# Products on 64x64 quarters of TensorE, with 128-row sums in two rounds

## The reference

```python
x = x + conv(_gn(x))          # relu(out_w @ (sigmoid(mask_w x) * relu(info_w x)))
t = tokens(x)
n = _ln_t(t)                  # query, key, value; elu+1; KV = K^T V; message @ Wm; norm
h = relu(concat(n, msg) @ W1) @ W2
t = t + n + layernorm(h)      # attention and MLP
probs = softmax(_ln_t(t) @ gate_w + gate_b)      # top 2 of 8 experts
for e in range(8):
    out += cw[:, e] * (gelu(_ln_t(t) @ W1[e] + b1[e]) @ W2[e] + b2[e])
result = t + out
```

## Time and profile before

| | |
|---|---|
| median of three runs | 1174.82 us (1172.48 to 1178.27) |
| span of the profiled execution | 1171.7 us |
| TensorE matmul busy | 1058.5 us, 90% |
| VectorE, ScalarE, GpSimd busy | 63%, 55%, 31% |
| granted TensorE clock, mean | 0.985 |
| a turn with all stages | 138.2 us |

### The profile page before, as it was taken

One profiled execution on the slowest core, in us unless ns is written; L12 is line 12 of the kernel. 1 busy time (PEld: TensorE's weight loads), 2 busy tenths in 40 slices (PEclk: granted clock), 3 DMA queues, 4 the chain that ended last, 5 costly groups with the idle time before them and its releaser, 6 DMA issues.

```text
span 1171.7 us, 16823 instructions
## 1 busy us (share of the span) xinstructions
PE 1058.5 (90%) x6646; PEld 442.3 (38%) x6646; DVE 740.2 (63%) x1529; ACT 641.8 (55%) x866; POOL 361.7 (31%) x280
## 2 busy tenths in 40 slices
PE   4798589979999899988999899998999989998898
PEld 1453244323533245332453235432453324532232
DVE  5744745686647875587664966468764886556344
ACT  3345355654566556664556546556556555665454
POOL 0000031333323333333232333133332342324465
PEclk9989889999999999999999999999999999999999
DMA  5000086007700284005810068000850039200760
GB/s 157 6 1 1 1 179 149 3 22 173 169 1 19 54 189 104 1 19 112 185 50 1 19 149 198 1 19 19 194 134 1 18 69 201 42 1 19 179 145 23
DMA packets 15597, 88.62 MB, mean 76 GB/s; under 512 B 3488, under 2 KB 6816, under 8 KB 11424
## 3 DMA queue, kind: packets, MB, share of 16 engines
q1 hardware_dynamic: 15520, 87.57, 32.3%
HBM read 78.12 MB, written 9.44 MB: 75 GB/s over the span
## 4 chain that ended last, share of the span: by engine, by line
PE 74%; DVE 12%; ACT 9%; issue 3%; DMA 1%; DVEq 0%; POOL 0%; POOLq 0%; SPq 0%
PE HP L847 15%; PE HP L861 14%; ACT H L992 5%; PE R L646 5%; PE R L621 4%; PE R L610 4%; PE R L699 3%; PE R L717 2%; PE R L708 2%; PE R L786 2%; PE R L795 2%; PE R L788 2%; PE R L861 2%; PE R L675 2%; DVE TM L1355 2%
## 5 line engine op out<-in xcount | busy, mean ns | idle before, releaser
L1044 POOL TENSOR_TENSOR XB<-TM,XB 128x512 f32<-128x512 f32 x254 | 323.0, 1286 | 658.5 <-DVE TM L1355 658.5
L992 ACT ACTIVATE H<-HP,W 128x1024 f32<-128x1024 f32 x224 | 243.0, 1116 | 205.7 <-PE HP L847 205.1
L1355 DVE SCALAR_TENSOR_TENSOR TM<-HP,B2S,CWB 128x512 f32<-128x512 f32 x224 | 163.2, 742 | 207.1 <-PE HP L861 196.3
L847 PE MATMUL HP<-XF,W1E 64*128 64x512 f32 x1024 | 269.9, 630 | 19.3 <-DVE TM L1355 18.5
L861 PE MATMUL HP<-H,W 128*64 128x512 f32 x896 | 233.1, 616 | 18.0 <-ACT H L992 18.0
L847 PEld LDWEIGHTS HP<-XF,W1E 64*128 64x128 f32 x1024 | 84.1, 187 | 143.9 <-DVE TM L1355 71.0
L861 PEld LDWEIGHTS HP<-H,W 128*64 128x64 f32 x896 | 48.5, 135 | 171.2 <-ACT H L992 116.3
L1156 DVE SCALAR_TENSOR_TENSOR BIG<-R,T 128x512 f32<-128x512 f32 x112 | 69.5, 681 | 20.9 <-PE R L610 20.8
L930 ACT ACTIVATE T<-R 128x512 f32<-128x512 f32 x96 | 57.4, 598 | 39.8 <-PE R L646 31.4
L958 ACT ACTIVATE T<-R,MINUS 128x512 f32<-128x512 f32 x64 | 41.4, 688 | 27.3 <-PE R L708 24.4
L1243 DVE SCALAR_TENSOR_TENSOR BIG<-T,R 128x512 f32<-128x512 f32 x64 | 41.8, 684 | 21.6 <-ACT T L958 21.6
(11 more groups left out here) (179 smaller groups left out, 1411.3 us busy)
## 6 DMA issues: line engine op xcount, KB each, us to landing
CWB<-gates_hbm SPq DMA_DIRECT2D x32, 1536.0 KB, 20.4
CWB<-gates_hbm SPq DMA_DIRECT2D x32, 512.0 KB, 6.6
out<-XB SPq DMA_DIRECT2D x15, 512.0 KB, 3.0
X<-x SPq DMA_DIRECT2D x14, 512.0 KB, 3.8
XF<-x SPq DMA_DIRECT2D x2, 512.0 KB, 6.1
gates_hbm<-RT SPq DMA_DIRECT2D x16, 64.0 KB, 1.6
W<-wpack SPq DMA_DIRECT2D x1, 968.0 KB, 4.9
W1E<-w1e SPq DMA_DIRECT2D x1, 512.0 KB, 7.4
```

What stands on the lines that cost most here:

```text
L847: last = mm(HP[u % BATCH][:, half(k)], W1E[img(k), e, :], XF[img(k), 1 - par, s, half(c)], start=True, stop=True)
L992: f(activated(b, u).rearrange("p k t -> p (k t)"), HP[u % BATCH][:, :], ACT.Gelu, bias=col(B1E + e))\
L1044: nc.gpsimd.tensor_tensor(acc, TM[:, u % BATCH, :], acc, ALU.add).then_inc(acc_done, 1)
L1355: v.scalar_tensor_tensor(out=TM[:, u % BATCH, :], in0=sums_of(b, u), scalar=B2S[:, e % 2, e // 2:e // 2 + 1], in1=CWB[:, s, e, half(c)], o ...
```

## The change

All of first_layer, second_layer, conv_out, hidden, hidden_out, message and last centring go to 64x64 quarters of the array, with four products side by side. A sum over 128 rows is now made in two rounds: in the first, each 64-row half of the operands goes to one of the two column halves; in the second, it goes to the other, and adds onto what the first left. Both row halves add into the same place in different rounds, so TensorE itself waits with a semaphore (y_first, oc_first, ho_first, h_first) for the end of the first round before the second. A "Y" in the list becomes an "A" (first round) and a "B" (second round); conv_out becomes conv_out and conv_sum, the second piece of hidden becomes hidden_1 and hidden_sum, hidden_out becomes hidden_out and result. The stages of ScalarE and VectorE that follow them have moved to the new names. The message and the last centring leave the zero blocks out: two quarters per piece, crossed. The constant that opens the query's sums runs on quarters too. The gate product is split by piece, with its weights turned for piece 1. In the last group second_layer has two buffers in place of four.

The core of the diff:

```diff
-    ("low_1.0", "YY", 0, 2), ("high_1.1", "", 0, 0), ("high_1.0", "HH", 2, 0), ("conv_out.1", "YY", 0, 2),
-    ("conv_out.0", "", 0, 0), ("centre_1.1", "", 0, 0), ("first_unit", "", 0, 0), ("finish_1", "", 0, 0),
-    ("centre_1.0", "", 1, 0), ("rstd_1", "HH", 0, 0), ("norm_1.0", "", 1, 1), ("norm_1.1", "Y", 0, 2),
-    ("weights_1", "Y", 0, 0), ("features_1.0", "H", 0, 0), ("features_1.1", "H", 2, 0),
+    ("low_1.0", "AABB", 0, 2), ("high_1.1", "", 0, 0), ("high_1.0", "HH", 2, 0), ("conv_out.1", "AA", 0, 2),
+    ("conv_out.0", "", 0, 0), ("conv_sum.1", "", 0, 0), ("conv_sum.0", "BB", 0, 0), ("centre_1.1", "", 0, 0), ("first_unit", "", 0, 0), ("finish_1", "", 0, 0),
+    ("centre_1.0", "", 1, 0), ("rstd_1", "HH", 0, 0), ("norm_1.0", "", 1, 1), ("norm_1.1", "AA", 0, 2),
+    ("weights_1", "BB", 0, 0), ("features_1.0", "H", 0, 0), ("features_1.1", "H", 2, 0),
...
-    ("attended.0", "", 0, 0), ("attended.1", "H", 0, 0), ("message.1", "", 0, 0), ("message.0", "Y", 0, 1),
-    ("variance_2", "HY", 0, 0), ("rstd_2", "Y", 1, 0), ("spread_2", "", 1, 2), ("norm_2.0", "HH", 1, 0),
+    ("attended.0", "", 0, 0), ("attended.1", "H", 0, 0), ("message.1", "A", 0, 0), ("message.0", "B", 0, 1),
+    ("variance_2", "AHB", 0, 0), ("rstd_2", "AB", 1, 0), ("spread_2", "", 1, 2), ("norm_2.0", "HH", 1, 0),
     ("hidden_0.0", "", 0, 0), ("norm_2.1", "", 0, 0), ("hidden_0.1", "", 0, 1), ("hidden_1.0", "", 0, 0),
-    ("hidden_1.1", "Y", 0, 0), ("hidden_out.1", "", 0, 0), ("hidden_out.0", "YH", 0, 0),
-    ("variance_3", "", 0, 1), ("rstd_3", "HYY", 3, 1), ("spread_3", "", 1, 1), ("norm_3.0", "HH", 0, 0),
-    ("centre_4.0", "", 0, 0), ("norm_3.1", "Y", 0, 0), ("centre_4.1", "YH", 0, 0),
-    ("variance_4", "HYY", 0, 2), ("rstd_4", "", 1, 2), ("spread_4", "", 0, 0), ("norm_4.0", "", 0, 0),
+    ("hidden_1.1", "", 0, 0), ("hidden_sum.0", "", 0, 0), ("hidden_sum.1", "A", 0, 0), ("hidden_out.1", "B", 0, 0), ("hidden_out.0", "A", 0, 0), ("result.1", "H", 0, 0), ("result.0", "B", 0, 0),
+    ("variance_3", "", 0, 1), ("rstd_3", "AHBAB", 3, 1), ("spread_3", "", 1, 1), ("norm_3.0", "HH", 0, 0),
+    ("centre_4.0", "", 0, 0), ("norm_3.1", "A", 0, 0), ("centre_4.1", "ABBH", 0, 0),
+    ("variance_4", "AHBAB", 0, 2), ("rstd_4", "", 1, 2), ("spread_4", "", 0, 0), ("norm_4.0", "", 0, 0),
...
+                def conv_out(turned, slots):
...
+                    for s in slots:
+                        if turned:
+                            pe.wait_ge(oc_first[s], a + 1)
+                        else:
+                            pe.wait_ge(prod_done[s], at(a * 4 + 4, LAST))
                         for h in range(2):
...
                 def by_feature(s, c, src, weights):
 
-                    return mm(R[s][:, half(c)], weights, src[:, s, half(c)], start=True, stop=True)
+                    for r, k in crossed(c):
+                        last = mm(R[s][img(k), half(c)], weights[img(r), img(r)], src[img(r), s, half(c)], start=True, stop=True)
+                    return last
...
                         for k in range(2):
-                            mm(R[s][:, half(k)], W1X[img(k), :], XN[img(k), s, half(c)], start=True, stop=False)
-                        for k in range(2):
-                            mm(R[s][:, half(k)], W1G[img(k), :], T1[img(k), s, half(c)], start=False, stop=True)\
-                                .then_inc(h_ps[s], 1)
+                            for n in range(2):
+                                last = mm(R[s][img(n), half(k)], W1X[img(k), img(n)], XN[img(k), s, half(c)], start=True, stop=False)
+                        if c == 0:
+                            hidden_sum(c, s)
+                        else:
+                            last.then_inc(h_first[s], 1)
...
-                def second_layer(u):
+                def second_layer(u, turned):
 
                     s, e, c = unit(u)
-                    pe.wait_ge(gelu_done, b * US + u + 1)
-                    if last_group(b):
-                        if u < FREE:
-                            pe.wait_ge(cwt_done, b + 1)
-                        else:
-                            pe.wait_ge(comb_done, b * US + u + 1 - FREE)
-                    for k in range(2):
-                        last = mm(sums_of(b, u)[img(k), :], w("w2e")[:, C * e:C * e + C], activated(b, u)[:, k, :],
-                                  start=True, stop=True)
-                    last.then_inc(y_ps, 1)
+                    if turned:
+                        pe.wait_ge(y_first, b * US + u + 1)
+                    else:
+                        pe.wait_ge(gelu_done, b * US + u + 1)
+                        if last_group(b):
+                            if u < BATCH:
+                                pe.wait_ge(cwt_done, b + 1)
+                            else:
+                                pe.wait_ge(comb_done, b * US + u + 1 - BATCH)
+                    for h in range(2):
+                        for k in range(2):
+                            r = k ^ h ^ turned
+                            last = mm(sums_of(b, u)[img(k), h, :], w("w2e", img(r))[:, C * e:C * e + C],
+                                      activated(b, u)[img(r), k ^ c, HALF * h:HALF * h + HALF], start=(turned == 0), stop=(turned == 1))
+                    last.then_inc(y_ps if turned else y_first, 1)
...
-                    **slotwise("conv_out", conv_out), **slotwise("centre_1", lambda slots: squares(1, slots)),
+                    **slotwise("conv_sum", conv_out), **slotwise("centre_1", lambda slots: squares(1, slots)),
```

More of the change, by code:

```diff
@@ L303, in build @@
         y3_done = sems("y3_done")
+        h_first = sems("h_first")
+        ho_first = sems("ho_first")
         h_ps = sems("h_ps")
@@ L411, in turn @@
                 return
-            at_step = {step: US - TAIL[column].count(step) for step in (FIRST, SECOND)}
+            at_step = {step: US - TAIL[column].count(step) for step in (FIRST, SECOND, OPEN, CLOSE)}
             for entry in SCHEDULE:
@@ new lines, in hidden, with hidden_sum @@
+                        if c == 0:
+                            hidden_sum(c, s)
+                        else:
+                            last.then_inc(h_first[s], 1)
+                def hidden_sum(c, s):
+                    if c == 1:
+                        pe.wait_ge(h_first[s], a + 1)
+                    for k in range(2):
+                        r = k ^ c
+                        for n in range(2):
+                            last = mm(R[s][img(n), half(k)], W1G[img(r), img(n)], T1[img(r), s, half(c)], start=False, stop=True)
+                        last.then_inc(h_ps[s], 1)
```

138 lines of the change are left out of this document (82 added, 56 removed), and 23 rows, old and new, of tables (OPENING, SCHEDULE).

## The result

The changed kernel takes 1270.83 us (median of four runs, 1269.75 to 1273.42) against 1173.81 on the same chip: ratio 1.0824, with a 95% interval from 1.08 to 1.0848. It is slower, as forecast, but by 97 us and not by 37; the time lies well above the range. The profiled execution spans 1271.6 us (before 1171.7), at a mean granted TensorE clock of 0.955 (before 0.985).

A forecast was written before the change was run, and what follows sets the result against it. TensorE's order was taken to bound the kernel, except in routing. Waits of 3.1 us a turn (21.7 over seven), convolution 10.2 and ends 5.1 added 37 us: forecast 1212 us, range 1184 to 1234.

The forecast's parts named there:

- the self-wait: Where B follows A with nothing between, TensorE waits for its own result: 0.3 us taken, bounds 0 to 0.5.
- the MLP: Spread_2 to variance_3: waits for relus and for squares of result.0 cost 2.5 us a turn, bounds 2.0 to 3.0.
- the message: Kv_values to variance_2: half the columns, then ScalarE's squares become the limit; gain 0.8 us, or 0.4 without overlap.
- the last centring: Spread_3 to variance_4: halved columns save 1.7 us, but H waits for the first B's combine; no gain.
- variance_2: Variance_2 to its spread: second-round order costs 0.4 us a turn, since VectorE's root hides part.
- rival of exposed weight loads: Each of 64 rounds pays 0.17 us for weight loads, 11 a turn, 76 in all: 1288 us; chance 0.05.
- Variance_3: Variance_3 to its spread: H starts 0.43 us later behind A, plus a self-wait; cost 0.65 a turn.
- Variance_4: Variance_4 to its spread: same delay of H and self-wait as in variance_3; cost 0.65 us a turn.
- Convolution: Convolution to next experts: VectorE's input additions wait behind combines that wait for BB; cost 1.7 us, six times, 10.2.
- The opening: Before the first expert step: waits in conv_out and hidden against a shorter message; cost 1.5 us, bounds -2 and 5.
- The ends: Last turns: four pairs where HH and YY stand alone lose 0.9 us each, 3.6; last group's pairs net 0.
- the dearest by waits: Rival: self-waits cost 0.8 us, not 0.3, and convolution and MLP reach upper bounds: 1232 to 1245; chance 0.05.

The follow-up runs named there:

- the mended kernel: Changed kernel with second-round and first-layer orders mended, early groups' convolution and MLP outputs and last group's second layer in one round: 1198.45 us, ratio 1.0208 to before.

## Why the prediction was right in sign and wrong in size

**Right.** The direction, and its reason: TensorE no longer sets the end where ScalarE and VectorE deliver between rounds. By its own steps: the self-wait (0.3 taken, 0.31 and 0.32 measured), the MLP (2.5, measured 2.63; hidden_1.1 idle 0.49, hidden_out.1 idle 1.23 and variance_3 idle 0.75 for squares, at the three places it named), the message (-0.8, measured -1.0; its quarters of two pieces do overlap: the first of the second piece start at 800.67, 0.11 after the last of the first), the last centring (0, measured 0 with the list of the change), variance_2. Rounds of 256 columns stream at full speed, in the last group 0.43 apart:

```profile
1207.48 0.64 PE L912 MATMUL R<-BIG,W 64*64 64x256 f32 x8
1207.91 1.07 PE L893 MATMUL HP<-XF,W1E 64*64 64x512 f32 x8
```

so the rival of exposed weight loads is refuted. The rule of the Trainium skill behind that rival (TensorE: Matmul & The Clock Gate, Part 3, The mechanism), that a weight load overlaps only where the row group differs, is not borne out here as it stands: these rows leave no time for a load in the round. The same section also lets a load go ahead that targets the background weight buffer, and with that the rows agree.

**Variance_3, 0.65 taken, 2.5 measured.** The step said that H starts 0.43 later "since A stands ahead of it, the gelu and the last A with it". It asked when the *last* A has its gelu, not when the *first* has. Before, the first step there was an H, which waits for no gelu, and the copies (1.84) and the gelu of the next Y ran under it. With A in front, 1.65 us of ScalarE's copies and gelu lie bare, and H, whose gelu the last A needs, stands behind. With H in front again the stretch takes 5.27 and not 6.84. The rows for it were on the table: the list and ScalarE's copies. Variance_4 has the same order with a gelu that is nearly there in time (A waits 0.22): 1.0 against 0.65.

**Convolution, 1.7 taken, 3.3 measured.** The place and its price were right: without GpSimd beside it, it is 1.9. The term that was missing is the price of an addition, taken as 0.69 from the earlier trace rows. That row's addition ran alone. Those of the changed kernel run right behind the combines, and so beside GpSimd's adds that these combines release, and two of them take 1.34 and 1.77. The kernel before has such a row, an addition beside GpSimd's add:

```profile
703.67 1.06 DVE L1163 TENSOR_TENSOR X<-X,T 128x512 f32<-128x512 f32 x1 [1.41 <-ACT T L924]
702.91 1.28 POOL L1044 TENSOR_TENSOR XB<-TM,XB 128x512 f32<-128x512 f32 x1
```

The step took the duration from the row that suited, without asking what ran beside it and what would after the move.

**The clock, no term.** Steady turns of before run at full clock (1.00). The sum priced waits in us at that clock and let nothing follow from them. After, most turns lose 1.0 to 1.3 once or twice to a stretch at half clock: 150.0 to 150.3 where the stretches at full clock add up to 147.7. Over the span, mean clocks of 0.955 and 0.985 mean some 114 and 35 us at half clock (twice the missing share of each span), of which the openings, at 0.80 and 0.92, have some 67 and 25.

**The opening, 1.5 taken with bounds -2 and 5, 14.8 measured.** The bounds were set without walking OPENING, though it has no expert steps: each round there is a bare wait for two more steps of other engines. One round in two stages takes 10.7 off.

**The ends.** The pairs of the last turn cost 5.38 for 4.35, near the forecast (0.9 each). The last group was forecast at 0 with waiting pairs at 4.05; they take 4.29, and the gap, a wait for code, and the clock behind it add 4.1, which nothing before showed.

**The sum.** Taken per turn with the convolution 4.8, measured 9.5 and 2.3 more by the clock. Of the 60 us that were missing, the opening has some 13, variance_3 13, the clock in the turns 14, the convolution 10 and the last group 6; variance_4 and routing have most of the rest. Of the rivals the dearest by waits gave 1232 to 1245; the one nearest in time, 1288, has a cause that the rows above refute. The price of a self-wait and the MLP were good; that the sum per turn of the places left, 2.3 in the mended kernel, is small is no test of it, since the orders differ. What failed was the walk along the order: which gelu the first step needs, what runs beside an addition, a stretch without experts, and a clock that fell behind some of the waits.

## What to carry to other kernels

When a step is split in two behind a wait, ask of every place in the order what the *first* instruction behind each stage now needs, and when the engine that delivers it gets to it in its own list; a step that needed nothing from others is worth most there, and should stay in front. Split where no second round is forced (here the last centring and the query's constant, 1% faster), and price a forced round before taking it: here one, even with other work laid between, ate what its part gained. A duration taken from a row holds for what ran beside it in that row, and stretches without cover (an opening, a last group) are to be walked by themselves. More and smaller products are also more code, and the traces here show the engine waiting for it.

## What the runs showed of the hardware

VectorE's additions of two SBUF operands and GpSimd's adds keep each other out. The four behind the convolution of the kernel after, one by one:

```profile
761.02 1.28 POOL L1099 TENSOR_TENSOR XB<-TM,XB 128x512 f32<-128x512 f32 x1 [8.67 <-DVE TM L1412]
761.52 1.34 DVE L1220 TENSOR_TENSOR X<-X,T 128x512 f32<-128x512 f32 x1
762.24 1.76 POOL L1099 TENSOR_TENSOR XB<-TM,XB 128x512 f32<-128x512 f32 x1
762.78 1.77 DVE L1220 TENSOR_TENSOR X<-X,T 128x512 f32<-128x512 f32 x1
```

Alone an addition takes 0.64 to 0.69 and an add 1.27 to 1.30. Here the first addition ends 0.55 after the first add, the second add 1.15 after that addition, and the second addition 0.55 after that add: each has all but some 0.13 us of its work behind the end of the one that began before it. In the kernel before the addition above also ends 0.55 after the add beside it (704.74 and 704.19). And GpSimd's add of one column, 0.19 by itself, takes 0.57 when it starts in an addition, and ends 0.04 after it. The Trainium skill (SBUF — State Buffer, Who interferes with whom) says that a VectorE instruction with two SBUF inputs contends with a GpSimd instruction that reads SBUF, and that the port pair they share is an exclusive lock. The trace agrees, by these ends.

A wait of TensorE on its own result costs 0.31 to 0.32 us where nothing stands between two rounds. Eight quarter matmuls of 256 columns take 0.43, so two rounds cost the same stream as one full-array step. And TensorE's busy time says little here: a turn of the mended kernel has 127.9 busy against 129.7, though the steps and changes of shape that it sheds were counted at 8.0. A record is longer than the distance to the next start (1.07 for 0.86 above), so changes of shape and short self-waits can disappear in it.
